# Threshold search: GpSimd marks two of eight tiles, two weight units run ahead of the search, and x's moments run inside it

## The reference

```python
# block 1, attention-like, on the context h (4, 512, 128)
sim = jnp.einsum('bhnd,bhmd->bnm', Q, K) / (jnp.sqrt(jnp.float32(d)) * H)   # 4 x 512 x 512
k = max(1, int(n * TOP_K_RATIO))                    # 153 of 512
threshold = jax.lax.top_k(sim, k)[0][:, :, -1:]     # the 153rd largest value of each row
A_learned = jax.nn.sigmoid(sim) * (sim >= threshold)
A_learned = (A_learned + jnp.swapaxes(A_learned, -1, -2)) * 0.5
x = x + tanh(g_xattn[0]) * ((1 - gamma) * layernorm(x) + gamma * A_learned)
# block 2: y = silu(q(z) @ q(w_gate).T) * (q(z) @ q(w_up).T), then q(y) @ q(w_down).T
# q cuts blocks of 32 values to a shared power of two and few mantissa bits
```

## Time and profile before

| | us |
|---|---|
| median of 3 runs | 1795.15 (1793.97 to 1795.43) |
| the profiled execution's own time | 1792.18 |
| its span | 1790.3 |
| first marks of the search | 40.54 |
| last instruction of `search` ends | 350.95 |

### The profile page before, as it was taken

The page is one execution under the profiler, slowest core; times in us unless marked ns, Lnnn a source line. Parts: engine busy times, 40 slices in busy tenths (PEclk is TensorE's granted clock), DMA queues, the critical chain, the costliest instruction groups (busy, mean ns, idle before and its releaser), DMA issues. The chain is left out here.

```text
span 1790.3 us, 30925 instructions
## 1 busy us (share of the span) xinstructions
PE 1459.2 (82%) x10394; PEld 767.9 (43%) x10395; DVE 1050.4 (59%) x1689; ACT 1016.6 (57%) x1551; POOL 789.5 (44%) x719
## 2 busy tenths in 40 slices
PE   6666666586888969999997306999999999999994
PEld 2445444462444424444443203444444444444442
DVE  3899999787999968888873824050641411460000
ACT  4999999924555537777774412444444444344441
POOL 3000000025777628888886164343544444454342
PEclk9677877888999979999998757999999999999997
DMA  9410100000000000000000475243533431531213
GB/s 337 154 43 30 48 25 1 30 1 1 1 1 1 1 1 3 3 3 3 2 3 16 171 298 176 36 119 81 170 102 103 117 83 38 161 100 29 36 24 106
DMA packets 49259, 118.86 MB, mean 66 GB/s; under 512 B 5536, under 2 KB 5792, under 8 KB 48576
## 3 DMA queue, kind: packets, MB, share of 16 engines
q1 hardware_dynamic: 34832, 88.53, 14.5%
q0 software_dynamic: 8176, 18.65, 5.4%
q10 hardware_dynamic: 6144, 10.28, 2.0%
HBM read 84.21 MB, written 37.43 MB: 68 GB/s over the span
## 5 line engine op out<-in xcount | busy, mean ns | idle before, releaser
L1638 PE MATMUL PS<-R 128*128 (+1 forms) x1872 | 433.0, 381 | 9.0 <-issue 7.9
L1792 DVE TENSOR_SCALAR R<-wring 128x1024 f16<-128x1024 f32 x56 | 61.4, 1107 | 382.2 <-PE PS L1661 350.8
L429 ACT ACTIVATE R<-R 128x512 bf16<-128x512 f32 x448 | 278.7, 709 | 11.1 <-PE PS L449 4.3
L1638 PEld LDWEIGHTS PS<-R 128*128 128x128 f16 x1872 | 179.4, 98 | 218.4 <-issue 20.3
L1828 POOL TENSOR_TENSOR R<-R 128x512 f32<-128x512 f32 x78 | 114.1, 1462 | 293.8 <-ACT R L1736 182.9
L449 PE MATMUL PS<-R,ident_b 128*128 128x256 bf16 (+1 forms) x1056 | 169.5, 322 | 85.0 <-ACT R L429 81.0
L1661 PE MATMUL PS<-R 128*128 (+1 forms) x936 | 214.9, 379 | 1.2 <-ACT R L1748 1.2
L1052 DVE TENSOR_REDUCE R<-PS 128x1 f32<-128x512 f32 x256 | 166.5, 685 | 44.6 <-PE PS L1234 41.9
L1030 POOL TENSOR_TENSOR R<-R 128x512 f32<-128x512 f32 x128 | 166.6, 1301 | 28.3 <-ACT R L1157 12.4
L1157 ACT ACTIVATE R<-PS 128x512 f32<-128x512 f32 x256 | 144.4, 599 | 40.9 <-PE PS L1248 40.3
L449 PEld LDWEIGHTS PS<-R,ident_b 128*128 128x128 bf16 x1056 | 115.1, 121 | 117.1 <-ACT R L429 91.6
(11 more groups left out here) (269 smaller groups left out, 2511.8 us busy)
## 6 DMA issues: line engine op xcount, KB each, us to landing
wring<-in_L_ffn_w_kernel_dram SPq DMA_DIRECT2D x48, 512.0 KB, 5.3
slot_rows<-R SPq DMA_DIRECT2D x1, 10023.0 KB, 40.3
R<-slot_rows ACTq DMA_DIRECT2D x39, 257.0 KB, 2.7
R<-in_L_ffn_w_kernel_dram SPq DMA_DIRECT2D x16, 512.0 KB, 5.8
wring<-in_L_ffn_wo_kernel_dram SPq DMA_DIRECT2D x16, 512.0 KB, 4.7
R<-in_L_ffn_wo_kernel_dram SPq DMA_DIRECT2D x16, 512.0 KB, 4.5
X<-in_x_dram SPq DMA_DIRECT2D x4, 1024.0 KB, 9.5
R<-in_L_ffn_w_up_dram SPq DMA_DIRECT2D x4, 1024.0 KB, 10.4
```

Of the source, the lines that this page charges most:

```text
L429: nc.scalar.activation(marks[:, j * S:(j + 1) * S], SIM[:, tile * S:(tile + 1) * S], ACT.Sign, bias=cfloat[:, tile:tile + 1], scale=-1.0). ...
L1638: mm = nc.tensor.matmul(bank[2 * half + g], ZT[n][:, (4 * pz + k) * P:(4 * pz + k + 1) * P], weights(place, at), start=(i % 12 == 0), stop ...
```

## The change

- `ACT_MARKS` falls from 7 to 6. GpSimd marks tiles 6 and 7 of each half (`pool_search`): per tile one instruction forms (value - candidate) x -2^126 in fp32 into `far` (in `wring`), a wait follows, and a second one bounds it to -1 .. 1 as bf16 into `marks`. VectorE's mark and `ident_2` go.
- `pe_search` folds tiles 4 to 7 with eight matmuls of 256 columns, after a wait for GpSimd's marks.
- GpSimd waits before both tiles for the candidate and for the second fold part of the half before.
- Of the small instructions of `search`, L517 becomes a scalar_tensor_tensor with a tile of -1.0 as second input, L540 a tensor_tensor with a broadcast input.
- Weight units 0 and 1 (`EARLY`) are quantized before the search, in a space of their own; their raw loads are issued ahead of x's. The other ten run in halves 8 to 57. Turns of PE and ACT follow the list `TURN_AT`. Units 2 to 5 are loaded before the zero fill.
- Moments of x, two tiles per half, go into halves 0 to 7, variance into half 8, the power to GpSimd in half 10, the coefficients into half 12. GpSimd applies s1 and s2 to one tile of x in every second half from 16 to 46.

```diff
-ACT_MARKS = 7
+ACT_MARKS = 6
+POOL_MARKS = 2
+HUGE = 2.0 ** 126
...
+        far = [wring[:, 512 * n:512 * n + 512] for n in range(2)]
...
+        def unit_space(u):
+            if u < EARLY:
+                return (R2[:, 8708:10756], marks_f, (R2[:, 10756:11780] if u else R3[:, 2 * UNIT:2 * UNIT + UNIT // 2]).bitcast(BF16),
+                        *(R2[:, 11780 + 64 * n:11844 + 64 * n] for n in range(4)))
...
             sp.dma_start(par[:, 4:5], gamma_raw.partition_broadcast(P)).then_inc(par_in, 16)
+            sp_weights(sp, 0, 2)
             for b in range(NB):
...
+        WEIGHTS_AT = 8
+        TURN_AT = [1, 3] + [WEIGHTS_AT + 5 * u + 5 for u in range(10)]
...
                     if h < HALVES:
                         pe.wait_ge(marked, h * ACT_MARKS + (ACT_MARKS if q else 4))
                         if q:
-                            pe.wait_ge(marked_dve, h + 1)
+                            pe.wait_ge(marked_pool, (h + 1) * POOL_MARKS)
...
-                    if q and h < HALVES:
-                        fold((7, 8), ident_2)
-                        mm = fold((4, 7), ident_b[:])
-                    else:
-                        mm = fold((4 * q, 4 * q + 4), ident_b[:])
-                    mm.then_inc(fold_ps, 1)
+                    fold((4 * q, 4 * q + 4), ident_b[:]).then_inc(fold_ps, 1)
...
         def dve_a(v):
-            v.wait_ge(x_in, 64)
-            with v.Fori(0, NT) as t:
-                dve_moments(v, t)
-            dve_ln_var(v, 0, 0)
-            dve_ln_scale(v, 0)
+            for u in range(EARLY):
+                for k in range(5):
+                    dve_weights(v, u, k)
...
-                nc.vector.tensor_scalar(keep[:, g], cnt[:, g], float(S - 2 * TOPK), -1.0, ALU.is_le,
-                                        ALU.mult).then_inc(keep_step, 1)
+                nc.vector.scalar_tensor_tensor(out=keep[:, g], in0=cnt[:, g], scalar=float(S - 2 * TOPK), in1=minus,
+                                               op0=ALU.is_le, op1=ALU.mult).then_inc(keep_step, 1)
...
-                    nc.vector.tensor_scalar(near[:, g], key[:, g], bit[:, n + 2:n + 3], None,
+                    nc.vector.tensor_tensor(near[:, g], key[:, g], bit[:, n + 2:n + 3].broadcast_to([P, HALF]),
                                             ALU.bitwise_xor).then_inc(near_step, 1)
...
-            mark(0)
-            for u in range(12):
-                for k in range(5):
-                    mark(5 * u + k + 1)
-                    search(5 * u + k)
-                    dve_weights(v, u, k)
...
+            for h in range(HALVES):
                 search(h)
+                moments(h)
+                if 0 <= h - WEIGHTS_AT < 50:
+                    dve_weights(v, EARLY + (h - WEIGHTS_AT) // 5, (h - WEIGHTS_AT) % 5)
...
+        def pool_search(pool):
+            pool.wait_ge(sim_sb, NT)
+            pool.wait_ge(raw_used, EARLY)
+            for h in range(HALVES):
+                pool.wait_ge(cand_ready, h + 1)
+                if h:
+                    pool.wait_ge(fold_ps, 2 * h)
+                for j in range(ACT_MARKS, HALF):
+                    tile, done = h % 2 * HALF + j, h * POOL_MARKS + j - ACT_MARKS
+                    if done > 1:
+                        pool.wait_ge(marked_pool, done - 1)
+                    nc.gpsimd.tensor_scalar(far[done % 2], SIM[:, tile * S:(tile + 1) * S],
+                                            cfloat[:, tile:tile + 1], -HUGE, ALU.subtract, ALU.mult).then_inc(apart, 1)
+                    pool.wait_ge(apart, done + 1)
+                    nc.gpsimd.tensor_scalar(marks[:, j * S:(j + 1) * S], far[done % 2], 1.0, -1.0,
+                                            ALU.min, ALU.max).then_inc(marked_pool, 1)
+                if h == NT // 2 + 2:
+                    pool_ln(pool, 0)
+                if 16 <= h < 16 + 2 * NT and h % 2 == 0:
...
+                    nc.gpsimd.tensor_scalar(xt, xt, s1[:, t:t + 1], s2[:, t:t + 1], ALU.mult, ALU.add).then_inc(lin, 1)
...
             sp_load(sp)
+            sp_weights(sp, 2, 6)
             sp_zero(sp)
-            sp_weights(sp)
+            sp_weights(sp, 6, 12)
```

More of the change, by code:

```diff
@@ L121, in bass_flamingo @@
         bit = R3[:, 5844:5876].bitcast(I32)
-        ident_2 = R3[:, 5880:5944].bitcast(BF16)
-        marks = R3[:, 6144:8192].bitcast(BF16)
+        minus = R3[:, 5944:5952]
+        marks_f = R3[:, 6144:8192]
+        marks = marks_f.bitcast(BF16)
+        far = [wring[:, 512 * n:512 * n + 512] for n in range(2)]
         A = R1[:, 0:8192]
@@ L430, in act_search @@
                                          bias=cfloat[:, tile:tile + 1], scale=-1.0).then_inc(marked, 1)
-                if h >= 6 and (h - 6) % 5 == 0 and (h - 6) // 5 < 11:
-                    act_weights(act, (h - 6) // 5)
-            act_weights(act, 11)
+                if h - 1 in TURN_AT:
+                    act_weights(act, TURN_AT.index(h - 1))
             act.wait_ge(raw_used, 12)
@@ L482, in dve_a @@
             v.wait_ge(coef_ready, 3)
[L483 to L493, removed]
+            v.wait_ge(wb_ready, EARLY)
+            v.wait_ge(bit_step, 36)
             v.wait_ge(id_ready, 2)
             v.wait_ge(sim_sb, NT)
-            nc.vector.tensor_scalar(ident_2, ident_b[:], 2.0, None, ALU.mult).then_inc(bit_step, 1)
-            v.wait_ge(bit_step, 36)
             nc.vector.tensor_copy(gone, key).then_inc(cand_ready, 2)
@@ L543, in search, with moments @@
                     nc.vector.tensor_copy(near[:, g], key[:, g]).then_inc(near_step, 1)
-            mark(0)
-            for u in range(12):
-                for k in range(5):
-                    mark(5 * u + k + 1)
-                    search(5 * u + k)
-                    dve_weights(v, u, k)
-            for h in range(60, HALVES):
-                if h + 1 < HALVES:
-                    mark(h + 1)
+            def moments(h):
+                if h < NT // 2:
+                    for t in (2 * h, 2 * h + 1):
+                        if t % TPB == 0:
+                            v.wait_ge(x_in, 16 * NB)
+                        dve_moments(v, t)
+                elif h == NT // 2:
+                    for part in range(2):
+                        dve_ln_var(v, 0, part)
+                elif h == NT // 2 + 4:
+                    v.wait_ge(ln_pow, 2)
+                    nc.vector.scalar_tensor_tensor(out=nmr[:], in0=lnt[:, 0, :], scalar=-0.5, in1=rstd[:],
+                                                   op0=ALU.mult, op1=ALU.mult).then_inc(ln_ready, 1)
+                    v.wait_ge(ln_ready, 1)
+                    nc.vector.tensor_scalar(s1, rstd[:], coef[:, 0:1], 1.0, ALU.mult, ALU.add).then_inc(coef_ready, 1)
+                    nc.vector.tensor_scalar(s2, nmr[:], coef[:, 0:1], None, ALU.mult).then_inc(coef_ready, 1)
+            for h in range(HALVES):
                 search(h)
+                moments(h)
+                if 0 <= h - WEIGHTS_AT < 50:
+                    dve_weights(v, EARLY + (h - WEIGHTS_AT) // 5, (h - WEIGHTS_AT) % 5)
             nc.vector.tensor_tensor(key, key, gone, ALU.bitwise_xor).then_inc(fin_step, 1)
@@ L602, in dve_a @@
                     dve_moments(v, tile)
[L604 to L609, removed]
+        def pool_search(pool):
[17 more added lines that the diff above has]
+                if 16 <= h < 16 + 2 * NT and h % 2 == 0:
+                    t = h // 2 - 8
+                    if t == 0:
+                        pool.wait_ge(coef_ready, 5)
+                    xt = X[:, t * D:(t + 1) * D]
+                    nc.gpsimd.tensor_scalar(xt, xt, s1[:, t:t + 1], s2[:, t:t + 1], ALU.mult, ALU.add).then_inc(lin, 1)
         def parts(ap, n):
@@ L680, in raw_loads, with sp_weights @@
             return 16 * (1 if u < 2 else (u - 2) // 4 + 1)
-        def sp_weights(sp):
-            for u in range(12):
+        def sp_weights(sp, first, end):
+            for u in range(first, end):
                 if u >= 6:
```

40 lines of the change are left out of this document (18 added, 22 removed).

## The result

| | us |
|---|---|
| before, median of 4 runs | 1794.93 |
| changed, median of 4 runs | 2037.12 (2034.99 to 2039.18) |
| ratio | 1.1356, 95% interval 1.1342 to 1.1371 |
| profiled execution, and its span | 2035.16, 2033.3 |

The kernel is 242 us slower. The prediction said slower, by 56 us, and its range ended at 1888.

A forecast was written before the change was run, and what follows sets the result against it. ACT bounds the kernel before; afterwards 50 halves with weights take 292 us, 14 on GpSimd's loop 66, extras 10: 368 against 311, +57, plus 1.5 for the start. Forecast 1851 us, range 1818 to 1888.

The forecast's parts named there:

- What GpSimd's marks cost alone: GpSimd's two marking instructions per tile at 0.76 and 0.68 us: a block of two tiles 3.05, a half 4.7.
- What bounds the kernel before: In the search ACT is the bound, busy 299.5 of 310 us; VectorE 14 us behind; GpSimd empty.
- The loop: GpSimd's block, second fold part and hand-offs can't overlap: 3.05 + 1.4 + 0.2, rounded to 4.7 us per half.
- The second instruction: GpSimd's bounding instruction per tile, fp32 to bf16: taken as 0.68 us, between 0.612 and 0.762.
- The exclusion: VectorE instructions with two SBUF inputs and GpSimd instructions don't overlap, in either order; 1.23 us passes counted too, reduces not held.
- How a half runs: Walk through a half with weights: VectorE's short instructions held by GpSimd's in turn, then its piece holds GpSimd; 5.84 us average.
- D + block: Length of a half with weights: end of VectorE's piece, D (3.55 or 2.3), plus GpSimd's 3.05 us.
- k = 1: Half whose VectorE weight piece has two passes, 2.29 + 1.23, D 3.55 with the hand-off: 6.6 us, as for k = 2.
- k = 3: Half whose VectorE weight piece ends at D = 2.3: 5.35 us.
- The rest of the sum: Search start 1.5 us later; extras on GpSimd 10: 6 for 16 instructions on x, 3 power, about 1 variance and coefficients.
- Rival 2: VectorE keeps GpSimd out of its whole run, halves of 9.15 us, 2017 in all; 6 in 100.
- Rival 1: GpSimd's marks hardly held by VectorE, so the loop rules: 1784, or 1758 to 1816 by fold clock; 11 in 100.

The follow-up runs named there:

- experiment 1: Kernel before, plus 24 GpSimd tensor_scalar instructions (12 forms) ahead of its search, VectorE idle: subtract/times 2.00 us, add/times 0.69; whole run 1808.84 us, not compared.
- experiment 2: Changed kernel with the marks put back (ACT seven tiles, VectorE one), moved weights and moments kept: 1792.83 us, ratio 1.000 to the kernel before.
- experiment 7: Changed kernel with VectorE's weight instructions of units 2 to 11 cut to 64 of 2048 columns: 1966.15 us, ratio 1.0958.
- experiment 3: Changed kernel with GpSimd's first instruction per tile as add/times on a negated candidate, instead of subtract/times: 1853.94 us, ratio 1.0332.
- experiment 8: Changed kernel with add/times as GpSimd's first instruction and weight instructions of units 2 to 11 cut to 64 of 2048 columns: 1765.95 us, ratio 0.9847.
- Experiment 9: Changed kernel, subtract/times kept, with GpSimd's first instructions of both tiles moved ahead of the wait for the fold: 1914.47 us, ratio 1.0674.

## Why the prediction was wrong

The step that failed is the first term of "What GpSimd's marks cost alone": "The first of its two instructions per tile is the form of L609: fp32 in and out, a scalar per row, 0.762 us." Shape, types and the row scalar are those of L609; the operations are not, and experiment 1 shows that they set the price: 2.00 against 0.69 to 0.77. I gave this instruction no upper bound at all, though no row of the trace before showed a tensor_scalar with subtract on GpSimd; for its partner I did give both ends. The range 1818 to 1888 rested on that. (It rests on loose arithmetic besides: the terms listed for 1825 to 1882 give 1812 to 1894 when added up, 1830 to 1872 as a root of squares.)

The trace before does show subtracts on GpSimd, of two tensors instead of a row scalar: L631, 1.152 at least, and L1836, which writes fp16, beside the multiply L1828:

```profile
L1828 POOL TENSOR_TENSOR R<-R x78: 1255/1262/9123, 1089.6 to 1761.5; 128x512 f32<-128x512 f32 x78
```

```profile
L1836 POOL TENSOR_TENSOR R<-R x78: 1151/1155/1970, 1099.5 to 1763.4; 128x512 f16<-128x512 f32 x78
```

So subtraction as such isn't slow there; the tensor_scalar with a row scalar is. A tensor_tensor as first instruction was not tried in the marks.

Point by point:
- **What bounds the kernel before**: right. With the marks put back and the rest moved, the time is the same to 0.1% (experiment 2).
- **The loop**, block + second fold part + hand-offs: right in its shape. Said 4.7; with 2.00 it is 5.35 + 1.9 + 0.3 = 7.5, and 7.5 was measured with and without passes beside it (experiment 7). With the fast form 4.73 in halves 0 to 7 (experiment 3), and 4.31 without passes (experiment 8).
- **The second instruction** (0.68) is 0.61, and the fold is 1.87 in the changed kernel, at a mean clock of 0.63: the halves grew longer and the clock fell from 0.75. That is the cold end of the bounds, 0.5 over the value taken.
- **The exclusion**: there, but under-priced by a third or more. The prediction put 5.84 - 4.7 = 1.1 us per half on it; measured are 8.98 - 7.52 = 1.5 in the changed kernel (the PE clock is 0.63 with and without passes, so the clock doesn't explain it) and 6.11 - 4.31 = 1.8 with the fast form, where the clock differs (0.70 and 0.90) and its part was not separated. "Don't overlap, in either order" doesn't hold for L616: VectorE's four short instructions and the start of L738 ran inside it.
- **How a half runs**, "VectorE was held in its short instructions by each GpSimd instruction in turn": wrong for the changed kernel, where L506 has a median of 0.167 and all but a few pass freely, partly right for the fast form (L533 0.56 on average). So D + block, with the right price 3.55 + 5.35 = 8.9 for k = 1 and 2.3 + 5.35 = 7.65 for k = 3, is 9.85 and 8.9 in the trace: the pass doesn't start with the end of the block but inside the next. L616 at 2 us and more was also named as a sign of being right; it came, but from its own length and not from a wait.
- **The rest of the sum**: start +1.5 said, +2.5 measured (42.4 against 39.9); x's sixteen, the power and the moments no visible share: in experiment 7 the halves with them (8 to 57, 7.52) are as long as those without (7.50, 7.55).

In numbers, with 50 and 14 halves: the loop went from the 4.86 of before to 7.5, 64 x 2.64 = 169; the passes add 73 by the counts, 71 by experiment 7; the start 2.5. The sum is 244 against 242 measured. The forecast had (4.7 - 4.86) x 64 = -10 for the loop and 57 for the passes.

So the direction was right for a smaller reason. With 2.00 for 0.76 and nothing else altered, the prediction's own walk through a half gives (2 x 8.9 + 2 x 7.65 + 7.6) / 5 = 8.14 us (k = 0 being 1.65 + 5.35 + 0.6), its loop 5.35 + 1.4 + 0.2 = 6.95, a search of 50 x 8.14 + 14 x 6.95 + 10 = 514 and 1997 in all. So this term is 146 of the 186 us by which the forecast missed; the other 40 lie almost all in halves 8 to 57, which took 8.98, with the pass inside the block and the cold fold; how much each costs was not separated.

The near hit of experiment 3 (1854 for 1851) is in part luck: the loop is shorter than said (4.31 for 4.7, with a warmer clock), the passes cost more (1.8 for 1.1 us per half), and the pieces that should be long are the short ones. Experiment 9 says that half of the loss, 123 us, came from where the slow instruction stood. Rival 2, priced at 2017, was near the time but not the cause: GpSimd's instructions got in between VectorE's, none took over 3 us. Rival 1, GpSimd's marks unheld, is close to what experiment 8 makes by taking the passes away (with the fast form and most of VectorE's work left out), at 1766, inside its 1758 to 1816; ACT is busy 267 of 282 us there, so the loop and ACT are nearly level.

## What to carry to other kernels

An engine's price for an instruction belongs to its operations as much as to its shape: where the trace has the shape with other operations, the bound above is open until it has been timed alone. Where two engines share one buffer, write down the loop through it before anything else and move whatever doesn't touch the buffer ahead of the wait: 37 us here with the fast form, 123 with the slow one. Work given to GpSimd beside VectorE's passes is not free even when GpSimd is empty: 1.5 to 1.8 us per half here.

## What the hardware showed that I had not expected

- GpSimd's tensor_scalar on 128x512 fp32: subtract/times 2.00 to 2.07 us, is_lt/subtract 2.00 to 2.02, subtract or is_lt alone 1.56 (all with a row scalar), add/times and multiply/add with a row scalar and a constant 0.69, multiply/add with two row scalars 0.77, two constants or min/max 0.61 to 0.62. All with VectorE idle. A tensor_tensor subtract takes 1.15 (L1836), a multiply 1.26 (L1828). Why one is slow and the other not is open.
- The slow instruction leaves VectorE's short two-input instructions alone (L506, 0.17 at 66.02, inside L616), while the fast one holds them (L509, 0.59 at 174.50, inside L628). A long pass that starts inside L616 costs it nothing if it is L738 (209.52), and 0.97 us if it is L744 (219.37). Why was not tried.
- After a pass whose successor waits for its result the waiting engine gets in: L619 at 210.31 ends 0.47 after L738, and L740, which follows, takes 1.52 where 1.23 is its least. The Trainium skill, SBUF — State Buffer, section Who interferes with whom, says in my words that whoever issues first has the shared ports for its whole instruction. The trace agrees for L619 behind L738 and for L631 behind L767 (2.68); it doesn't for L616, which issued first and held nothing, and not for the run of eight in the earlier trace rows, where none waits for the one before it and GpSimd got in behind the last alone.
- The PE clock was higher the denser the search: a mean of 0.63 at 7.5 to 9 us per half, 0.70 at 6.1 (halves 8 to 57), 0.90 at 4.3, with the same matmuls. A fold of eight matmuls took 1.87 at one end (about that in 55 of 64 second parts of the changed kernel) and 1.05 at the other (under 1.2 in 49 of 64 in experiment 8). So a loop that gets shorter may get shorter once more by the clock; no run separates the two.
